# A six-stage decoder on one core: first work of the cross attention placed in the last turns of the attention, and that attention's value masks two chunks later

## The reference

```python
# block 1: attention, 16 heads of width 8, with a table of relative values added to the result,
# then a layer norm of its own and the residual
# block 2: cross attention, 16 heads of width 64
q = (x @ Wq + bq); k = (ctx @ Wk + bk); v = (ctx @ Wv + bv)
scores = q @ k.T * scale + NEG_INF * (1.0 - causal)
ctx = softmax(scores) @ v
out = ctx @ Wo + bo
```

## Time and profile before

| | |
|---|---|
| three timed executions | 1650.61, 1657.35, 1658.14 us; median 1657.35 |
| the profiled execution | 1648.13 us, its span 1645.4 us |
| mean granted TensorE clock | 0.95 of full |
| TensorE matmul, weight load | 90% and 58% of the span |
| VectorE, ScalarE, GpSimd | 65%, 53%, 45% |
| l0_attn | from 0 to about 140.1 us of the span |
| l0_xattn | from there to about 340 us |

### The profile page before, as it was taken

One profiled execution on the slowest core, in us unless ns is written; L12 is line 12 of the kernel. 1 busy time (PEld: TensorE's weight loads), 2 busy tenths in 40 slices (PEclk: granted clock), 3 DMA queues, 4 the chain that ended last, 5 costly groups with the idle time before them and its releaser, 6 DMA issues.

```text
span 1645.4 us, 41074 instructions
## 1 busy us (share of the span) xinstructions
PE 1482.1 (90%) x17022; PEld 950.0 (58%) x17022; DVE 1069.6 (65%) x1723; ACT 870.4 (53%) x1783; POOL 744.4 (45%) x670
## 2 busy tenths in 40 slices
PE   6887999989999789857699999999999999879998
PEld 3555888765444446524466666666666666555554
DVE  4885555532432368776588888888888888724554
ACT  2442333345655324315477777777777777743333
POOL 4665211100000147767477777877777777000000
PEclk8877999999999889987899999999999999989999
DMA  4003000023211240334655465565645554504310
GB/s 118 1 2 106 2 2 2 2 72 99 65 39 26 57 88 1 67 72 99 128 124 129 124 129 124 124 134 126 121 129 128 123 128 109 120 1 91 63 60 16
DMA packets 62539, 129.54 MB, mean 79 GB/s; under 512 B 15793, under 2 KB 38066, under 8 KB 59186
## 3 DMA queue, kind: packets, MB, share of 16 engines
q1 hardware_dynamic: 62354, 126.92, 33.1%
HBM read 100.22 MB, written 26.67 MB: 77 GB/s over the span
## 4 chain that ended last, share of the span: by engine, by line
PE 33%; POOL 11%; ACT 7%; DVE 3%; issue 2%; DMA 1%; SPq 0%; ACTq 0%; POOLq 0%; DVEq 0%
PE ps L1706 7%; POOL ARENA L1910 7%; PE ps L847 7%; PE ps L1690 5%; POOL ARENA L1916 3%; PE ps L859 3%; PE ps L1653 3%; ACT ARENA L1860 3%; PE ps L1644 2%; ACT ARENA L1838 2%; PE ps L1667 2%; ACT ARENA L1851 1%; ACT ARENA L1844 1%; DVE ARENA L1780 1%; PE ps L1715 1%
## 5 line engine op out<-in xcount | busy, mean ns | idle before, releaser
L1780 DVE TENSOR_REDUCE ARENA<-ps 112x2 f32<-112x1000 f32 x384 | 456.4, 1197 | 118.2 <-PE ps L1667 115.4
L1860 ACT ACTIVATE ARENA<-ps 125x448 f32<-125x448 f32 x768 | 378.4, 549 | 127.9 <-PE ps L1690 127.2
L1910 POOL TENSOR_TENSOR ARENA<-ARENA 64x500 f32<-64x500 f32 x192 | 264.1, 1376 | 104.9 <-ACT ARENA L1838 86.5
L107 POOL TENSOR_TENSOR rs<-rs,mhalf 128x1 f32<-128x1 f32 x96 | 57.9, 604 | 373.2 <-DVE rs L102 373.1
L847 PE MATMUL ps<-XT,ARENA 128*128 128x448 f32 x544 | 219.7, 548 | 0.0
L1690 PEld LDWEIGHTS ps<-ARENA 64*125 64x125 bf16 x3072 | 122.5, 134 | 133.6 <-ACT ARENA L1860 70.5
L1690 PE MATMUL ps<-ARENA 64*125 64x112 bf16 x3072 | 169.1, 228 | 19.8 <-ACT ARENA L1860 18.8
L1706 PE MATMUL ps<-ARENA 125*17 125x112 f32 x6144 | 185.4, 260 | 0.0
L1667 PE MATMUL ps<-ARENA 64*112 64x500 bf16 x768 | 152.7, 386 | 10.1 <-DVE ARENA L1780 9.7
L859 PE MATMUL ps<-ARENA 128*128 128x448 f32 x400 | 161.6, 539 | 0.0
L847 PEld LDWEIGHTS ps<-XT,ARENA 128*128 128x128 f32 x544 | 104.3, 194 | 99.2 <-issue 98.8
(11 more groups left out here) (228 smaller groups left out, 2141.8 us busy)
## 6 DMA issues: line engine op xcount, KB each, us to landing
ARENA<-key_parts SPq DMA_DIRECT2D x192, 187.5 KB, 4.3
ARENA<-in_ctxT SPq DMA_DIRECT2D x96, 250.0 KB, 3.8
key_parts<-ARENA SPq DMA_DIRECT2D x64, 375.0 KB, 2.7
ARENA<-token_weights SPq DMA_DIRECT2D x32, 512.0 KB, 5.5
ARENA<-in_L_ffn_W SPq DMA_DIRECT2D x1, 2048.0 KB, 9.9
ARENA<-query_parts SPq DMA_DIRECT2D x6, 192.0 KB, 6.9
ARENA<-in_c_ones SPq DMA_DIRECT2D x2, 562.5 KB, 14.3
ARENA<-in_L_attn_a SPq DMA_DIRECT2D x2, 512.0 KB, 5.4
```

The lines of the kernel that those rows point to most:

```text
L1780: e.tensor_reduce(mxp[0:112, b % 2, 2 * g:2 * g + 2, ch], ps[0:112, b1:b1 + 2, 0:500], AX, ALU.max) \
L1860: e.activation(Pb[0:KT, n % NP_, 448 * h:448 * h + 448], ps[0:KT, b1[h], 0:448], ACT.Exp, bias=0.0, scale=1.0).then_inc(exped.sem, 1)
L1910: e.tensor_tensor(T2[r:r + 64, :], T0[64 - r:128 - r, n % 2, :], sin[64 - r:128 - r, sl], ALU.mult) \
```

## The change

Two things.

- The value masks of the first attention run two chunks behind instead of one: VectorE's list goes over n = 0 to 5, with the masks of chunk n-2 behind the statistics of chunk n. For that the values get four PSUM banks (4 to 7) instead of two, queries and keys only the banks 2 and 3; the relative table's transposes move from chunk 3 to chunk 4, into the banks 2 and 3; and the products of the relative table move from ahead of the loop into its turn 1, on TensorE behind the scores of tile 2, on ScalarE behind the exponential of tile 0.
- The first cross attention's first queries, keys, values and constant row are made in the last turns of the first attention: TensorE does them behind its turn 17 (`front_pe`), VectorE and ScalarE take them out behind their turn 18. The transposes of the layer norm's tiles 13 to 15 use bank 1 alone. The constant row comes last of the four instead of first. The spreading of bv moves to turn 2 of the attention's loop, behind two other preparations.

```diff
-                    at[key] = 4 + ring % 3
+                    at[key] = 4 + ring % 3 if t < NT + 2 else 1
...
-                    for bk, wt, mm, cp in ((2 + 2 * (n % 2), wq, q_mm, q_cp), (3 + 2 * (n % 2), wk, k_mm, k_cp)):
+                    for bk, wt, mm, cp in ((2, wq, q_mm, q_cp), (3, wk, k_mm, k_cp)):
...
-                        bk = 6 + v % 2
+                        bk = 4 + v % 4
...
-                    if n == 3:
+                    if n == 4:
...
-                            bk = 4 + half
+                            bk = 2 + half
...
-                w.wait_ge(*v_cp(8))
-                w.wait_ge(*bias_cp(2))
-                for g in range(4):
...
                 for t in range(NT + 5):
                     if t + 1 < NT:
                         scores(t + 1)
+                    if t == 1:
+                        w.wait_ge(*v_cp(8))
+                        w.wait_ge(*bias_cp(2))
+                        for g in range(4):
...
+                    if t == NT + 1:
+                        stages[1].parts["front_pe"](e, w)
...
             def dve(e, w):
-                for n in range(5):
+                for n in range(6):
...
-                    if n:
+                    if n >= 2:
                         w.wait_ge(*par_in(1))
-                        for v in (2 * n - 2, 2 * n - 1):
+                        for v in (2 * n - 4, 2 * n - 3):
...
+                    if t == NT + 2:
+                        stages[1].parts["front_dve"](e, w)
...
+                    if t == 1:
+                        for g in range(4):
+                            w.wait_ge(*base_mm(g + 1))
...
+                    if t == NT + 2:
+                        stages[1].parts["front_act"](e, w)
...
+                e.tensor_copy(bvr, bv.unsqueeze(2).broadcast_to([128, 8, 128])).then_inc(bv_wide.sem, 1)
...
+            def front_pe(e, w):
+
+                w.wait_ge(*xw_in(len(loads)))
+                w.wait_ge(*one_set(1))
+                w.wait_ge(*bv_wide(1))
+                pe_queries(e, w, 0)
+                pe_keys(e, w, 0)
+                pe_values(e, w, 0)
+                w.wait_ge(*free[0])
+                for c in range(8):
+                    e.matmul(ps[:, 0, 0:128], bvr[:, c, :], wo[:, c, :], start=(c == 0), stop=False)
+                e.matmul(ps[:, 0, 0:128], one1[0:1, :], bo[0:1, :], start=False, stop=True).then_inc(xb_mm.sem, 1)
+                free[0] = xb_cp(1)
...
+            def front_dve(e, w):
+                dve_queries(e, w, 0)
+                dve_keys(e, w, 0)
...
+            def front_act(e, w):
+                act_values(e, w, 0)
                 w.wait_ge(*xb_mm(1))
                 e.copy(xb, ps[:, 0, 0:128]).then_inc(xb_cp.sem, 1)
-                values(0)
```

More of the change, by code:

```diff
@@ L292, in pe @@
                         scores(t + 1)
+                    if t == 1:
+                        w.wait_ge(*v_cp(8))
+                        w.wait_ge(*bias_cp(2))
+                        for g in range(4):
+                            w.wait_ge(*free[4 + g])
+                            for c in range(2):
+                                for b in range(2):
+                                    m = e.matmul(ps[64 * b:64 * b + 64, 4 + g, 256 * c:256 * c + 256], bT[0:112, 2 * g + c, :],
+                                                 Vb[0:112, b:B:2, 2 * g + c, 0:16], start=True, stop=True)
+                            m.then_inc(base_mm.sem, 1)
+                            free[4 + g] = base_cp(g + 1)
                     u = t - 1
@@ L400, in act @@
                         e.copy(kT[:, sl], ps[:, b0 + 1, :]).then_inc(k_cp.sem, 1)
[L401 to L404, removed]
                 for t in range(NT + 5):
+                    if t == 1:
+                        for g in range(4):
+                            w.wait_ge(*base_mm(g + 1))
+                            e.copy(base[:, :, 2 * g:2 * g + 2, :].rearrange("p t c n -> p c t n"),
+                                   ps[:, 4 + g, :].rearrange("p (c t n) -> p c t n", c=2, t=NT)).then_inc(base_cp.sem, 1)
                     u = t - 1
@@ L521, in prep_dve @@
                 e.tensor_copy(idb, ident[:, :]).then_inc(consts.sem, 1)
-            def pe(e, w):
[L524 to L549, removed]
@@ new lines, in pe_keys, with pe_values @@
+            def pe_keys(e, w, t):
+                for c in range(8):
+                    w.wait_ge(*free[K_BANK + c // 4])
+                    m = e.matmul(ps[:, K_BANK + c // 4, 112 * (c % 4):112 * (c % 4) + 112], wk[:, 128 * c:128 * c + 128],
+                                 ck[:, 2 * t:2 * t + 2, :], start=True, stop=True)
+                m.then_inc(k_mm.sem, 1)
+                free[K_BANK] = free[K_BANK + 1] = k_cp(t + 1)
+            def pe_values(e, w, t):
+                wr = wv.rearrange("p (c r d) -> p r c d", c=8, r=2)
+                for b in range(2):
+                    w.wait_ge(*free[V_BANK + b])
+                    for r in range(2):
+                        m = e.matmul(ps[64 * r:64 * r + 56, V_BANK + b, :], ck[:, 2 * t + b, :], wr[:, r],
+                                     start=True, stop=True)
+                    m.then_inc(v_mm.sem, 1)
+                    free[V_BANK + b] = v_cp(2 * t + b + 1)
@@ L551, in scores @@
+            def pe(e, w):
+                queries, keys, values = (lambda t, f=f: f(e, w, t) for f in (pe_queries, pe_keys, pe_values))
                 def scores(t):
@@ L598, in project @@
                     free[O_BANK] = joined(t + 1)
-                w.wait_ge(*xw_in(len(loads)))
-                w.wait_ge(*one_set(1))
-                w.wait_ge(*bv_wide(1))
-                w.wait_ge(*free[0])
-                for c in range(8):
-                    e.matmul(ps[:, 0, 0:128], bvr[:, c, :], wo[:, c, :], start=(c == 0), stop=False)
-                e.matmul(ps[:, 0, 0:128], one1[0:1, :], bo[0:1, :], start=False, stop=True).then_inc(xb_mm.sem, 1)
-                free[0] = xb_cp(1)
-                queries(0)
-                keys(0)
-                values(0)
                 for t in range(NT + 2):
@@ L650, in dve @@
+            def front_dve(e, w):
+                dve_queries(e, w, 0)
+                dve_keys(e, w, 0)
+            def dve(e, w):
+                queries, keys = (lambda t, f=f: f(e, w, t) for f in (dve_queries, dve_keys))
                 for t in range(NT + 2):
@@ L713, in act @@
                     if t + 1 < NT:
-                        values(t + 1)
+                        act_values(e, w, t + 1)
                     if t >= 2:
```

75 lines of the change are left out of this document (36 added, 39 removed).

## The result

| | before | the change |
|---|---|---|
| median of the executions timed side by side | 1656.07 us (4) | 1632.31 us (4) |
| lowest and highest | 1650.61, 1658.14 | 1629.23, 1639.73 |
| profiled execution (span) | 1648.13 (1645.4) | 1629.23 (1627.4) |

The ratio is 0.988, with a 95% interval of 0.9841 to 0.992: faster, and by more than the half per cent of the prediction. The sign and the places of the gain were right, the size was not. Timed again beside 17 executions of the kernel before (median 1649.17), the change had 1633.71 us over six: ratio 0.9903, 0.9876 to 0.993.

A forecast was written before the change was run, and what follows sets the result against it. VectorE and the chain through all engines paced the attention's loop, TensorE the cross attention's. Front 6.2 plus boundary 2.6 gave 8.8 us off a mean of 1653.6: 1645 us, range 1637 to 1656.

The forecast's parts named there:

- 1. gap, first to second projection: Front: four transposes at some 0.5 us each make the gap 2.0 us instead of 4.55, gain 2.5 us.
- 2. gap, second to third: Front: five transposes at 0.5 us make the gap 2.5 us instead of 6.7, gain 4.2 us.
- 3. relative table: Front: now between third and fourth projection, queries and keys wait for its copies, loss 1.2 us.
- 4. last projection to transposes: Front, up to the loop: TensorE waits for tile 0's shift, 7.8 us instead of 6.1, loss 1.7 us.
- 5. clock, second to fourth projection: Front: smaller gaps let projections run at a higher clock, gain 2.4 us, between a 3.0 loss and a 4.7 gain.
- boundary: Start of the cross attention's loop: 147.0 us instead of 151.15, gain 4.1 us before the clock fall.
- clock fall behind it: Behind the boundary: TensorE, with only three transposes in 3.3 us, falls to a slower clock, loss 1.5 us.
- the upper bound: Front's clock term: all projections as fast as the fourth, gain 4.7 us.
- some 0.5 us a tile: Front: estimated pace of transposes and their copies with two banks taking turns, giving gaps of 2.0 and 2.5 us.
- the holes close better: Rival: projections at 2.4 GHz, no boundary fall, no 7.5 us turn; 12.6 us plus up to 5.1, 1636 to 1641; chance 0.20.
- Given back: Rival: projections stay slow and waits run longer in the front, some 4 us gained in all, 1649.6 us; chance 0.20.
- locked: Rival: attention loop stays at 1.2 GHz, every other turn takes 7.5 us, net 2.7 us slower, 1656.3; chance 0.10.

The follow-up runs named there:

- e7: Kernel before with eight, three and five filler products in the holes of the front's chunks 2 and 3: 1645.1 us, ratio 0.9961.
- e2: The change with masks, banks and relative products of the front as before, so the boundary's half alone: 1644.3 us, ratio 0.9959.
- e5: The change with GpSimd's spreading of keys of tile t+2 waiting for VectorE's relative sum of tile t-3: 1630.46 us, ratio 0.9869.
- e9: The change with e3, e5 and e6 on top: 1628.8 us, ratio 0.9859.
- e3: The change with the products of the relative table back ahead of the loop: 1627.63 us, ratio 0.9863.
- e6: The change with eight filler products after every other group of the second cross attention's last turns: 1631.73 us, ratio 0.988.
- e4: Kernel before with filler products between transposes of chunks 2 and 3, five ahead of each chunk's first, one elsewhere: 1648.38 us, ratio 0.9981.

## Why the prediction was wrong in size

Point by point, measured between the first profiles of both kernels and between the second ones:

| term | forecast | first profiles | second profiles |
|---|---|---|---|
| 1. gap, first to second projection | 2.5 | 4.55 to about 0.97: 3.6 | 3.7 |
| 2. gap, second to third | 4.2 | 6.7 to 1.7: 5.0 | 5.0 |
| 3. relative table | -1.2 | -1.3 (26.40 to 27.66) | -1.3 |
| 4. last projection to transposes | -1.7 | -1.7 (31.29 to 39.14: 7.85, forecast 7.8) | -1.7 |
| 5. clock, second to fourth projection | 2.4 | 4.7 | 5.1 |
| first projection | 0 | 0.6 | 0.3 |
| boundary | 4.1 | 17.57 to 12.12: 5.4 | 19.71 to 12.87: 6.8 |
| clock fall behind it | -1.5 | -1.6 | 0 |
| sum | 8.8 | 14.7 | 17.9 |

The first projection is the same work in both kernels, and its L258 took 1.91 and 2.58 us in the two profiles of the change, 2.30 and 2.62 in those of before: that row is chance.

The front's losses came out to a tenth. The gains failed in three steps.

- **"I take 2.4, the middle of nothing and 4.7"** cost most. The clock has two levels, and with holes that short the second, third and fourth projection ran at 2.4 GHz in all profiles with the new front: the upper bound. e7 has the same by itself, 4.5 to 5.4 us. Term 5 should have been two cases with a chance each, not a mean.
- **"some 0.5 us a tile"** was mis-sized. The first two transposes of a chunk take 0.38 us together, as both banks are free, the next pair waits 0.25 for a copy, and the projection behind them needs only the first of their copies. Four tiles took 0.97 us, five 1.7, against 2.0 and 2.5: 1.9 us more gain.
- **"Before, TensorE's clock was 1.2 GHz at 141.13 and rose by 145.54, after 4.4 us of dense work"**, at the boundary: the sum took one instance of a thing with two. In the first profile of the change the slow stretch was over within the queries (3.29 us); in the second it lasted 3.75 us and into the keys, as forecast. The chain from tile 13's transpose to the mask took 2.7 us in both, not 3.3. And before itself is at 17.2 to 17.6 or at 19.7 to 20.0 us, of which the sum knew the first. Over all profiles the boundary is worth 5.3 us with the fall in it, in e2's time 4.9, where the forecast had 2.6.

"I expect the same fall" was half right: tile 1's queries took 3.13 to 3.29 us in the profiles of the change, e5 and e9, but 2.05 in those of its second profile, e2, e3 and e6. It is chance. But the forecast charged the full slow stretch at tile 0 and the fall at tile 1 together, where the profiles show the one shorter or the other absent.

A last step is the base. 8.8 was taken off 1653.6, the mean of four executions; over 17 and 23 executions before has medians of 1649.17 and 1651.82. So of the 12.7 us between 1645 and 1632.31, some 6 to 7 are the three steps (14.7 in the first profiles, 15.5 between the medians, against 8.8), 2 to 4 the base, and the rest spread, in part that of the first comparison's four and four.

The rival "the holes close better" has the mechanism (12.6 us without the long turns) and would have been the better forecast, though its 1636 to 1641 owes up to 5.1 us to long turns that are chance. "Given back" and "locked" did not: L375's wait is 1.59 us, where about 1 was forecast, inside a term 4 that came out as worked, and the loop is as long as before (59.5 and 62.1 us, before 64.3 and 59.6). VectorE's copy of bv in turn 2 took 0.69 us at 39.16, beside no GpSimd spreading, with the next input some 4 us away: cost nothing, as forecast. The text would have been wrong in kind, had the start of the cross attention's loop moved and the end not; between the first profiles the start moved 21.1 us (4.7 of them long turns) and the end 18.0.

## What to carry to other kernels

Where two engines alternate in short steps, holes on TensorE cost twice: once as waiting, and again in the dense work behind them at 1.2 GHz, here 10.9 us of front of which about half was each. Cost such a clock term as one of its two ends, with a chance each, and look at more than one profile of before: its boundary read 17.57 us in one and 19.71 in the next. And look for what else spreads the time (here 9.6 us at a far-off stage's end) before taking a baseline from four executions.

## What the runs showed of the hardware that was not expected

- The clock fell in e4 although TensorE had no idle above 0.69 us ahead of it; with the holes filled (e7) it stayed at 2.4 GHz.
- One drain of a pipeline, 1400 us into the program, takes 33.4 us at a clock of 1.00 or 43.0 at one of 0.59 for the same instructions, and at times something between (34.8, 38.5): up to twice what the whole boundary change is worth. What tips it is open.
- Filler products cost nothing that shows where TensorE waits anyway: e7 is 6.7 us faster than before with 39 more of them.
